# Decoder stage: the self-attention's small products placed beside the value products, its output projection one step later

## The chip, the cores and the metric

One core of a Trainium2 chip runs the whole program. The metric is device time in microseconds of one execution; the kernel before was timed in 3 runs, and a change is judged by the median.

## What is computed

The reference is a stack of four blocks over x (32 sequences of 32 rows, 256 wide) and a context of 257 rows a sequence. The change touches one part, the call `_L1_xattn_ref`: a decoder of six layers. Each layer does self-attention over the 32 rows (16 heads of 16, masked), adds and normalises, cross-attention to the context, adds and normalises, and a dense part of 256 to 1024 to 256 with ReLU, adds and normalises. In the reference's words, for a layer l:

```
x = layer_norm(x + mha(x, x, sa_w[l], sa_b[l], mask))
x = layer_norm(x + mha(x, ctx, ca_w[l], ca_b[l], None))
x = layer_norm(x + relu(x @ w1[l] + b1[l]) @ w2[l] + b2[l])
```

Everything is float32.

## The kernel before

`decoder_layers` (L2118) works on tiles of 128 rows, four sequences each: 8 tiles times 6 layers are 48 positions. A software pipeline runs over steps. In a step five parts work on different positions (L2179): `sa` (self-attention) on position step, `prep` (queries, keys and values of the cross-attention) on step - 1, `ca` (its scores, softmax, products) on step - 2, `out` (its projection) and `dm` (the dense part) on step - 3. So 51 steps; in the first three and the last three some parts are empty.

A step has eight units, u0 to u7. In every even unit PE does the scores of two units of four heads and sequences (L2359), DVE takes the row maximum from PSUM (`maxima`, L2454), ACT does four exponentials (`exponentials`, L2601), DVE forms reciprocal rates in the odd unit (`pair_rates`, L2460), POOL scales the probabilities (`scale`, L2539), and two units after its own each unit is transposed on PE (job T, L2371) and copied by ACT. In every odd unit PE multiplies a pair with the values (job PV, L2378), which DVE takes (`own_heads`, L2468).

Between these stand the jobs of the table `UNIT_JOBS` (L2133), each with the engine that evacuates its PSUM bank: `n`, `q`, `K`, `V`, `X` for prep (X, the last key's values, only in the first position of a layer), `Y` for out; `S0` transposes the input of self-attention, `S1q` and `S1k` are its queries and keys, `S2` its values, `S3` its scores, `S6` its products with the values, `S7` its output projection; `D0` to `D3` are the dense part: D0 transposes, D1 and D2 are the two halves of the first product, D3 is the second. All jobs, T and PV among them, go in one list in that order, T first in its unit and PV last (L2189). They share a ring of four PSUM banks, and a job waits for the evacuation of the job four before it (L2280):

```
o = ps[:, RING + n % RB]
if n >= RB:
    pe.wait_ge(s[evacuated[n - RB][0]], evacuated[n - RB][1])
```

Every engine does its part of this list in order, with its own work written between. DVE's loop (L2502): it first takes what it put off in the unit before (S3, D3 and PV), then the maximum in an even unit, then in u0 the unfinished norms, in u4 `self_shares` (sum, reciprocal, product and transpose of the self-attention's probabilities, L2493), in odd units the rates, then the jobs of the unit, then in u2 `own_queries` (L2478) and in u3 `self_shift` (mask, maximum, subtraction, L2486), then unfinished norms, save in u7. S2's evacuation (L2438) writes a masked copy of four times its size, and S1q's (L2432) one of eight times. A norm is `norm_statistics` (L2402), a root on POOL (`root`, L2535), and `norm_apply` (L2412). ACT's loop (L2609) takes in even units T and, save in u6, the first job behind it, then the exponentials, then the rest; in odd units its jobs; and in u3, behind these, the exponential of the self-attention (L2621). SP loads the next context tile in each step and the next layer's weights in groups, each behind the last use of the old ones (L2243).

The matmul forms differ: most products use the whole array (128x128). The scores use parts of 32 rows and 64 columns; S3 (L2330), S6 (L2338) and PV (L2386) use column strips of 32 ("128*32" in the profile), four at once.

Of the kernel before, what the change touches and what calls it, by code (L numbers as in the profile page):

```python
# [16 lines left out]
ACT = mybir.ActivationFunctionType  # L17
# [2100 lines left out]
def decoder_layers(E, A):  # L2118
# [8 lines left out]
    def k_job(i):  # L2127
        return ("K", (i // 2, i % 2), "act")

    def v_job(i):  # L2130
        return ("V", i, "dve")

    UNIT_JOBS = [  # L2133
        [("S0", None, "act"), k_job(0), v_job(0)],
        [("S1q", None, "dve"), k_job(1), ("S1k", None, "act"), ("n", None, "act")],
        [("q", None, "act"), v_job(1), ("Y", None, "dve"), ("S3", None, "dve")],
        [k_job(2), v_job(2)],
        [("D0", None, "act"), k_job(3), ("S2", None, "dve")],
        [("D1", 0, "act"), v_job(3), ("S6", None, "dve")],
        [("D2", 1, "act"), ("X", None, "act")],  # L2140
        [("S7", None, "dve"), ("D3", None, "dve")],
    ]
    PART = {"n": "prep", "X": "prep", "q": "prep", "K": "prep", "V": "prep", "Y": "out", "S0": "sa", "S1q": "sa", "S1k": "sa", "S2": "sa", "S3": "sa", "S6": "sa", "S7": "sa",
            "D0": "dm", "D1": "dm", "D2": "dm", "D3": "dm"}

    w = E.layer
# [8 lines left out]
    with ExitStack() as st:  # L2155
        s, handles = signals(st, nc, "layers", "job_done evac_dve evac_act scores_done max_ready exp_done "
                             "last_exp rates_ready scaled bias_ready shifted soft_done pT_ready qblk_ready h_sa h_ca h_dm var_ready added_eps power_ready dve_step "
                             "ctx0 ctx1 w_sa_qk w_sa_v w_sa_o w_ca_q w_ca_k w_ca_v w_ca_o w_dm")
# [5 lines left out]
        KT, V = sb("KT", [2, DC, GB * KW]), sb("V", [2, VC, D])  # L2164
# [5 lines left out]
        sa_sc, sa_pT, sa_attnT = sb("sa_sc", [16, LQ]), sb("sa_pT", [16 * LQ]), sb("sa_attnT", [DC, P])  # L2170
# [5 lines left out]
        NPOS = NL * NG  # L2176
        steps = []
        for step in range(NPOS + 3):
            at_part = {"sa": step, "prep": step - 1, "ca": step - 2, "out": step - 3, "dm": step - 3}  # L2179
            steps.append({part: pos if 0 <= pos < NPOS else None for part, pos in at_part.items()})  # L2180
        N = len(steps)

        def ca_unit(it):
            pos = it // U - 2
            if not 0 <= pos < NPOS:
                return None
            return it - 2 * U, pos, it % U // GB, it % GB

        jobs, at = [], {}  # L2189
        for step, parts in enumerate(steps):  # L2190
            for u in range(U):
                it = step * U + u
# [3 lines left out]
                for kind, arg, engine in UNIT_JOBS[u]:  # L2196
                    pos = parts[PART[kind]]
                    if pos is not None and (kind != "X" or pos % NG == 0):
# [14 lines left out]
        def jobs_in(it):  # L2213
            return by_unit.get(it, [])
# [19 lines left out]
        with nc.Block(no_gpsimd_drain=True) as blk:  # L2234
# [40 lines left out]
            def _(pe):  # L2275
                mm, tr = nc.tensor.matmul, nc.tensor.transpose

                def job(n, step, u, kind, arg, engine):
# [3 lines left out]
                    if kind in ("T", "PV"):  # L2282
                        (transposes if kind == "T" else values)(o, *ca_unit(arg)).then_inc(s["job_done"], 1)
                        return
                    pos = steps[step][PART[kind]]
                    tile = pos % NG
# [110 lines left out]
            def _(dve):  # L2397
# [14 lines left out]
                def norm_apply(kind, count, tile):  # L2412
                    y = ytmp[kind][:]
                    dve.wait_ge(s["power_ready"], count)
                    link(v.tensor_scalar(y, y, stats[kind][:, 6:7], stats[kind][:, 8:9], ALU.subtract, ALU.mult))
                    link(v.tensor_tensor(y, y, LN_ROWS[kind][:, 1], ALU.mult))
                    v.tensor_tensor(E.h[:, tile], y, LN_ROWS[kind][:, 2], ALU.add).then_inc(s["h_" + kind], 1)

                unfinished = []
# [73 lines left out]
                def self_shares(pos):  # L2493
                    dve.wait_ge(s["soft_done"], pos + 1)
                    link(v.tensor_reduce(sa_sum[:], sa_sc[:], AX.X, ALU.add))
                    link(v.reciprocal(sa_sum[:], sa_sum[:]))
                    link(v.tensor_tensor(sa_sc[:], sa_sc[:], sa_sum[:].unsqueeze(2).to_broadcast([P, 16, LQ]), ALU.mult))
                    v.transpose(sa_pT[:], sa_sc[:].rearrange("p h k -> p (h k)")).then_inc(s["pT_ready"], 1)
# [3 lines left out]
                for it in range(N * U + 1):  # L2502
                    step, u = it // U, it % U
                    for a in put_off:
                        take(*a)
                    put_off.clear()
                    if it % 2 == 0 and ca_unit(it):
                        maxima(*ca_unit(it))
                    if u == 0:
                        for a in unfinished:  # L2510
                            norm_apply(*a)
                        unfinished.clear()
                    if u == 4 and steps[step]["sa"] is not None:
                        self_shares(steps[step]["sa"])
                    if it % 2 and ca_unit(it - 1):
                        pair_rates(*ca_unit(it - 1))
                    for a in jobs_in(it):
                        if a[3] in ("S3", "D3", "PV"):
                            put_off.append(a)
                        else:  # L2520
                            take(*a)
                    if u == 2 and steps[step]["prep"] is not None:
                        own_queries(steps[step]["prep"])
                    if u == 3 and steps[step]["sa"] is not None:
                        self_shift(steps[step]["sa"])
                    if u != 7:
                        for a in unfinished:
                            norm_apply(*a)
                        unfinished.clear()

            @blk.gpsimd
            def _(pool):
                made = [0]

                def root(kind):  # L2535
                    power(E, pool, s, made[0], stats[kind][:, 8:9], stats[kind][:, 7:8], 1e-12)
                    made[0] += 1

                def scale(k, pos, cc, j):  # L2539

                    pool.wait_ge(s["rates_ready"], k // 2 + 1)
                    at = slice(2 * (j % 2), 2 * (j % 2) + 2)
                    nc.gpsimd.tensor_tensor(probs[:, cc, j // 2, at], probs[:, cc, j // 2, at], rates[:, cc, j // 2, at].unsqueeze(2).to_broadcast([P, 2, KW]), ALU.mult).then_inc(s["scaled"], 1)  # L2543

                for it in range(N * U + 1):
                    step, u = it // U, it % U
                    if u == 0 and step and steps[step - 1]["dm"] is not None:
                        root("dm")
                    if u == 2 and step < N and steps[step]["out"] is not None:
                        root("ca")  # L2550
                    if it % 2 and ca_unit(it - 1):
                        scale(*ca_unit(it - 1))
                        scale(*ca_unit(it))
                    if u == 7 and steps[step]["sa"] is not None:
                        root("sa")

            @blk.scalar
            def _(act):
                a = nc.scalar.activation
# [41 lines left out]
                def exponentials(k, pos, cc, j):  # L2601
                    act.wait_ge(s["max_ready"], k // 2 + 1)
                    if k >= U:
                        need_job(act, k + 1 - U, "T")
                    for r in range(4):
                        a(probs[:, cc, j // 2, r], ps[:, r, 0:KW], ACT.Exp, bias=negmax[:, cc, j // 2, r:r + 1], accum_out=totals[:, cc, j // 2, r:r + 1]).then_inc(s["exp_done"], 1)  # L2606
                    a(last_e[:, cc, j // 2], negmax[:, cc, j // 2], ACT.Exp).then_inc(s["last_exp"], 1)

                for it in range(N * U):  # L2609
                    step, u = it // U, it % U  # L2610
                    early = 0
                    if it % 2 == 0 and ca_unit(it):
                        early = (u != 6) + (jobs_in(it)[0][3] == "T")
                        for b in jobs_in(it)[0:early]:
                            take(*b)
                        exponentials(*ca_unit(it))
                    for b in jobs_in(it)[early:]:
                        take(*b)
                    if steps[step]["sa"] is not None and u == 3:
                        act.wait_ge(s["shifted"], steps[step]["sa"] + 1)  # L2620
                        a(sa_sc[:], sa_sc[:], ACT.Exp).then_inc(s["soft_done"], 1)  # L2621

        end_round(nc, handles)

# [1209 lines left out]
```

## Time and profile before

| | |
|---|---|
| median of 3 runs | 4272.2 us (4267.39 to 4278.87) |
| the profiled execution's own time | 4274.82 us |
| its span, first to last instruction | 4272.7 us |
| mean granted TensorE clock, share of full | 0.936 |
| busy: PE, DVE, ACT, POOL | 3751.7, 2537.8, 1808.4, 738.1 us |
| the decoder's stretch | about 725 to 2655 us of the span |

Busy time counts instructions; matmuls overlap, so the time that a job costs PE is read from its first start to the first start of the next job. "Idle before, releaser" is the time for which an engine stood still ahead of an instruction and what ended it. PEld is the weight load, which runs ahead of the matmul that uses it. A granted clock of 1.00 is 2.4 GHz, 0.50 is 1.2 GHz.

### The profile page before, as it was taken

Reading aid. Unit: us, or ns where it says so; the run is one execution under the profiler, and the core shown is the slowest. Engines: PE = TensorE matmul, PEld = TensorE weight load, DVE = VectorE, ACT = ScalarE, POOL = GpSimd, SP = SyncE. Lnnn points to the kernel's source line nnn. Section 1 sums busy time; section 2 is a strip of 40 time slices with the busy share of each in tenths; the row PEclk is TensorE's granted clock in tenths of the full one; section 3 lists DMA queues with packets and bytes.
Section 4 is the critical chain, followed back from the end, with each engine's and each line's share of the span. In section 5 each row is a group of like instructions: output and inputs, shape, how many; then the busy total and the mean of one; then the engine's idle time right before and its main releaser. Section 6 shows DMA issues by size and latency. Waiting matters only on the chain. (4 is left out here: it accounts for less than half of the span.)

```text
span 4272.7 us, 99175 instructions
## 1 busy us (share of the span) xinstructions
PE 3751.7 (88%) x40748; PEld 2830.3 (66%) x40748; DVE 2537.8 (59%) x5335; ACT 1808.4 (42%) x4979; POOL 738.1 (17%) x960
## 2 busy tenths in 40 slices
PE   7986995999999999999999997679678879889866
PEld 5765884677777777777777775568445569555535
DVE  4444213677777777777777774731257757346545
ACT  2221321445545455545555553212176736256522
POOL 1100101222222222222222222020121100000000
PEclk9998997999999999999999998879889979999977
DMA  5221386001101101111101100138544410000001
GB/s 175 91 76 52 109 303 221 31 31 43 61 31 47 56 32 52 51 36 47 61 29 45 61 21 12 40 131 297 208 142 150 154 35 1 27 31 31 11 3 49
DMA packets 141630, 329.30 MB, mean 77 GB/s; under 512 B 35512, under 2 KB 93304, under 8 KB 121984
## 3 DMA queue, kind: packets, MB, share of 16 engines
q1 hardware_dynamic: 138112, 314.57, 21.8%
q0 software_dynamic: 3072, 8.39, 0.6%
q8 instruction: 327, 5.36, 0.5%
q14 instruction: 119, 0.97, 0.1%
HBM read 286.98 MB, written 23.33 MB: 73 GB/s over the span
## 5 line engine op out<-in xcount | busy, mean ns | idle before, releaser
L2543 POOL TENSOR_TENSOR layers_probs<-layers_probs,layers_rates 128x512 f32<-128x512 f32 x384 | 399.9, 1063 | 906.8 <-DVE layers_rates L2466 906.8
L2570 ACT COPY layers_pT<-banks 128x512 f32<-128x512 f32 x384 | 227.9, 594 | 460.4 <-PE banks L2375 460.4
L2606 ACT ACTIVATE layers_probs<-banks,layers_negmax 128x256 f32<-128x256 f32 x768 | 354.1, 476 | 106.3 <-DVE layers_negmax L2458 106.2
L2311 PE MATMUL banks<-weights_a,ctx_tiles 128*128 128x256 f32 x1536 | 367.7, 382 | 27.5 <-ACT layers_KT L2583 27.5
L2304 PE MATMUL banks<-ctx_tiles,weights_a 128*128 128x512 f32 x768 | 364.8, 598 | 0.0
L2311 PEld LDWEIGHTS banks<-weights_a,ctx_tiles 128*128 128x128 f32 x1536 | 284.4, 190 | 112.1 <-issue 46.3
L2375 PE MATMUL banks<-const,layers_probs 128*128 128x128 f32 x1536 | 244.0, 282 | 2.9 <-POOL layers_probs L2543 2.8
L2375 PEld LDWEIGHTS banks<-const,layers_probs 128*128 128x128 f32 x1536 | 172.4, 142 | 106.5 <-issue 78.4
L2457 DVE TENSOR_REDUCE layers_negmax<-banks 128x4 f32<-128x1024 f32 x192 | 233.6, 1216 | 4.1 <-PE banks L2368 1.6
L2436 DVE COPY layers_V<-banks 128x512 f32<-128x512 f32 x192 | 132.4, 689 | 149.6 <-PE banks L2311 149.2
L2583 ACT ACTIVATE layers_KT<-banks,layers_key_bias 128x512 f32<-128x512 f32 x192 | 133.0, 693 | 154.1 <-PE banks L2304 153.9
L2304 PEld LDWEIGHTS banks<-ctx_tiles,weights_a 128*128 128x128 f32 x768 | 132.4, 192 | 93.8 <-issue 93.6
L2350 PE MATMUL banks<-layers_dm_nT,weights_b 128*128 128x128 f32 x1536 | 189.9, 278 | 0.6 <-ACT layers_dm_nT L2575 0.6
L2356 PE MATMUL banks<-weights_b,layers_hid 128*128 128x256 f32 x768 | 184.2, 385 | 4.5 <-ACT layers_hid L2598 4.2
L2350 PEld LDWEIGHTS banks<-layers_dm_nT,weights_b 128*128 128x128 f32 x1536 | 181.9, 194 | 0.9 <-ACT layers_dm_nT L2575 0.9
L2356 PEld LDWEIGHTS banks<-weights_b,layers_hid 128*128 128x128 f32 x768 | 141.8, 190 | 39.5 <-ACT layers_hid L2598 22.3
L2606 ACT ACTIVATION_READ_ACCUMULATOR layers_probs<-banks,layers_negmax 128x1 f32 x768 | 159.3, 207 | 0.0
L2368 PE MATMUL banks<-layers_KT,layers_qblk 32*64 32x256 f32 x3072 | 133.4, 403 | 0.0
L2386 PE MATMUL banks<-layers_pT,layers_V 128*32 128x64 f32 x6144 | 124.8, 222 | 9.2 <-ACT layers_pT L2570 7.7
L2886 PE MATMUL banks<-weights_a,ctx_tiles 128*128 128x512 f32 x256 | 128.8, 633 | 0.5
L2386 PEld LDWEIGHTS banks<-layers_pT,layers_V 128*32 128x32 f32 x6144 | 96.2, 110 | 49.6 <-issue 33.5
L2432 DVE SCALAR_TENSOR_TENSOR weights_a<-banks,layers_sa_cols,const 128x1024 f32<-128x1024 f32 x96 | 118.9, 1279 | 5.3 <-PE banks L2297 3.6
(707 smaller groups left out, 8126.9 us busy)
## 6 DMA issues: line engine op xcount, KB each, us to landing
ctx_tiles<-ctx_rel SPq DMA_DIRECT2D x48, 1024.0 KB, 5.7
weights_a<-in_L_w SPq DMA_DIRECT2D x44, 1024.0 KB, 5.6
l2x_B<-positions SPq DMA_DIRECT2D x32, 1280.0 KB, 5.8
weights_b<-in_L_w SPq DMA_DIRECT2D x32, 1024.0 KB, 6.4
ctx_tiles<-in_ctx SPq DMA_DIRECT2D x16, 1028.0 KB, 5.1
weights_c<-in_L_w SPq DMA_DIRECT2D x16, 1024.0 KB, 7.1
weights_b<-in_L_xattn_w SPq DMA_DIRECT2D x12, 1024.0 KB, 7.3
l0x_key_rows<-in_ctx_rows SPq DMA_DIRECT2D x32, 256.0 KB, 2.7
```

The source lines that it names most:

```text
L2304: last = mm(o, ca_wk[:, c, m * P:(m + 1) * P], E.ctx[:, tile % 2, c, 2 * i * KW:2 * (i + 1) * KW], start=c == 0, stop=c == DC - 1)
L2311: last = mm(o[:, b * D:(b + 1) * D], E.ctx[:, tile % 2, c, first:first + P], ca_wv[:, c], start=c == 0, stop=c == DC - 1)
L2350: last = mm(o[:, i * P:(i + 1) * P], dm_w1[:, c, m * P:(m + 1) * P], dm_nT[:, c], start=c == 0, stop=c == DC - 1)
L2356: last = mm(o[:, 0:D], hid[:, m], dm_w2[:, m], start=m == 0, stop=m == FC - 1)
L2368: last = mm(ps[64 * a:64 * (a + 1), r, 0:KW], qblk[rows, tile % 2, cc, j + a], KT[rows, tile % 2, cc, (j + a) * KW:(j + a + 1) * KW], star ...
L2375: last = tr(o[:, (KC * i + c) * P:(KC * i + c + 1) * P], probs[:, cc, j // 2, 2 * (j % 2) + i, c * P:(c + 1) * P], E.c("ident"))
L2386: last = mm(o[32 * r:32 * (r + 1), a * 64:(a + 1) * 64], V[:, pos % 2, KC * (j + a) + c, cc * P + 32 * r:cc * P + 32 * (r + 1)], pT[:, (k ...
L2457: link(v.tensor_reduce(peak, ps[:, 0:4, 0:KW], AX.X, ALU.max, negate=True))
L2543: nc.gpsimd.tensor_tensor(probs[:, cc, j // 2, at], probs[:, cc, j // 2, at], rates[:, cc, j // 2, at].unsqueeze(2).to_broadcast([P, 2, KW ...
L2570: nc.scalar.copy(pT[:, k % 4].rearrange("p t c x -> p (t c x)"), o).then_inc(s["evac_act"], 1)
L2583: last = a(KT[:, pos % 2, m, 2 * i * KW:2 * (i + 1) * KW], o, ACT.Identity, bias=key_bias[:, m:m + 1])
L2606: a(probs[:, cc, j // 2, r], ps[:, r, 0:KW], ACT.Exp, bias=negmax[:, cc, j // 2, r:r + 1], accum_out=totals[:, cc, j // 2, r:r + 1]).then_ ...
```

## The change

The table of jobs changes: S2 goes from u4 to u2, S3 from u2 to u3, S6 from u5 to u7, n from u1 to u2, q from u2 to u3, D3 ahead of S6 in u7, and S7 from u7 to u0 of the next step, behind K0, under a part name of its own, `sa_end` (position step - 1). S3 and S6 are now the last jobs ahead of the values' PV in u3 and u7. DVE puts S6 off as well; `own_queries` goes to u3, `self_shift` to u4, `self_shares` to u5 and behind the jobs of that unit; norms are finished in u7 too. POOL's root for the self-attention goes to u0, ACT's exponential of the self-attention to u5, behind T and ahead of the other jobs.

```diff
--- before.py
+++ after.py
@@ -2131,16 +2131,16 @@
         return ("V", i, "dve")
 
     UNIT_JOBS = [
-        [("S0", None, "act"), k_job(0), v_job(0)],
-        [("S1q", None, "dve"), k_job(1), ("S1k", None, "act"), ("n", None, "act")],
-        [("q", None, "act"), v_job(1), ("Y", None, "dve"), ("S3", None, "dve")],
-        [k_job(2), v_job(2)],
-        [("D0", None, "act"), k_job(3), ("S2", None, "dve")],
-        [("D1", 0, "act"), v_job(3), ("S6", None, "dve")],
+        [("S0", None, "act"), k_job(0), ("S7", None, "dve"), v_job(0)],
+        [("S1q", None, "dve"), k_job(1), ("S1k", None, "act")],
+        [("n", None, "act"), v_job(1), ("Y", None, "dve"), ("S2", None, "dve")],
+        [("q", None, "act"), k_job(2), v_job(2), ("S3", None, "dve")],
+        [("D0", None, "act"), k_job(3)],
+        [("D1", 0, "act"), v_job(3)],
         [("D2", 1, "act"), ("X", None, "act")],
-        [("S7", None, "dve"), ("D3", None, "dve")],
+        [("D3", None, "dve"), ("S6", None, "dve")],
     ]
-    PART = {"n": "prep", "X": "prep", "q": "prep", "K": "prep", "V": "prep", "Y": "out", "S0": "sa", "S1q": "sa", "S1k": "sa", "S2": "sa", "S3": "sa", "S6": "sa", "S7": "sa",
+    PART = {"n": "prep", "X": "prep", "q": "prep", "K": "prep", "V": "prep", "Y": "out", "S0": "sa", "S1q": "sa", "S1k": "sa", "S2": "sa", "S3": "sa", "S6": "sa", "S7": "sa_end",
             "D0": "dm", "D1": "dm", "D2": "dm", "D3": "dm"}
 
     w = E.layer
@@ -2176,7 +2176,7 @@
         NPOS = NL * NG
         steps = []
         for step in range(NPOS + 3):
-            at_part = {"sa": step, "prep": step - 1, "ca": step - 2, "out": step - 3, "dm": step - 3}
+            at_part = {"sa": step, "sa_end": step - 1, "prep": step - 1, "ca": step - 2, "out": step - 3, "dm": step - 3}
             steps.append({part: pos if 0 <= pos < NPOS else None for part, pos in at_part.items()})
         N = len(steps)
 
@@ -2510,23 +2510,22 @@
                         for a in unfinished:
                             norm_apply(*a)
                         unfinished.clear()
-                    if u == 4 and steps[step]["sa"] is not None:
-                        self_shares(steps[step]["sa"])
                     if it % 2 and ca_unit(it - 1):
                         pair_rates(*ca_unit(it - 1))
                     for a in jobs_in(it):
-                        if a[3] in ("S3", "D3", "PV"):
+                        if a[3] in ("S3", "S6", "D3", "PV"):
                             put_off.append(a)
                         else:
                             take(*a)
-                    if u == 2 and steps[step]["prep"] is not None:
+                    if u == 3 and steps[step]["prep"] is not None:
                         own_queries(steps[step]["prep"])
-                    if u == 3 and steps[step]["sa"] is not None:
+                    if u == 4 and steps[step]["sa"] is not None:
                         self_shift(steps[step]["sa"])
-                    if u != 7:
-                        for a in unfinished:
-                            norm_apply(*a)
-                        unfinished.clear()
+                    if u == 5 and steps[step]["sa"] is not None:
+                        self_shares(steps[step]["sa"])
+                    for a in unfinished:
+                        norm_apply(*a)
+                    unfinished.clear()
 
             @blk.gpsimd
             def _(pool):
@@ -2546,13 +2545,13 @@
                     step, u = it // U, it % U
                     if u == 0 and step and steps[step - 1]["dm"] is not None:
                         root("dm")
+                    if u == 0 and step < N and steps[step]["sa_end"] is not None:
+                        root("sa")
                     if u == 2 and step < N and steps[step]["out"] is not None:
                         root("ca")
                     if it % 2 and ca_unit(it - 1):
                         scale(*ca_unit(it - 1))
                         scale(*ca_unit(it))
-                    if u == 7 and steps[step]["sa"] is not None:
-                        root("sa")
 
             @blk.scalar
             def _(act):
@@ -2614,11 +2613,14 @@
                         for b in jobs_in(it)[0:early]:
                             take(*b)
                         exponentials(*ca_unit(it))
+                    if u == 5 and steps[step]["sa"] is not None:
+                        early = int(jobs_in(it)[:1] != [] and jobs_in(it)[0][3] == "T")
+                        for b in jobs_in(it)[0:early]:
+                            take(*b)
+                        act.wait_ge(s["shifted"], steps[step]["sa"] + 1)
+                        a(sa_sc[:], sa_sc[:], ACT.Exp).then_inc(s["soft_done"], 1)
                     for b in jobs_in(it)[early:]:
                         take(*b)
-                    if steps[step]["sa"] is not None and u == 3:
-                        act.wait_ge(s["shifted"], steps[step]["sa"] + 1)
-                        a(sa_sc[:], sa_sc[:], ACT.Exp).then_inc(s["soft_done"], 1)
 
         end_round(nc, handles)
 
```

## Rows read from the trace of the kernel before

**Rows 1.** Windows, one steady step: stretch, length, busy time (instructions) by engine, clock, DMA.

```profile
1513.53:1552.33 38.80, 38.19 (x449) 28.35 (x443) 30.01 (x67) 19.56 (x64) 10.79 (x15) 1.00 0.08 29
```

**Rows 2.** Waits, 760 to 2560 us: us in total, times, longest.

```profile
PE banks L2311 <- ACT layers_KT L2583: 27.5, 45, 0.6
```

**Rows 3.** Timeline of PE, part of a step: start, us, line, operation, instructions.

```profile
1526.87 1.03 PE L2320 MATMUL banks<-weights_a,layers_attnT 128*128 128x256 f32 x4
1527.83 1.07 PE L2330 MATMUL banks<-weights_a,layers_sa_k 128*32 128x256 f32 x16
...
1529.32 1.88 PE L2304 MATMUL banks<-ctx_tiles,weights_a 128*128 128x512 f32 x4
...
1537.79 1.95 PE L2350 MATMUL banks<-layers_dm_nT,weights_b 128*128 128x128 f32 x16
1540.36 1.99 PE L2311 MATMUL banks<-weights_a,ctx_tiles 128*128 128x256 f32 x8 [0.61 <-ACT layers_KT L2583]
1542.28 1.10 PE L2338 MATMUL banks<-layers_sa_pT,layers_sa_v 128*32 128x64 f32 x64
...
1543.76 0.69 PE L2368 MATMUL banks<-layers_KT,layers_qblk 32*64 32x256 f32 x16
...
1544.87 1.95 PE L2350 MATMUL banks<-layers_dm_nT,weights_b 128*128 128x128 f32 x16
1546.65 0.60 PE L2375 MATMUL banks<-const,layers_probs 128*128 128x128 f32 x4
1547.09 1.03 PE L2343 MATMUL banks<-weights_c,layers_sa_attnT 128*128 128x256 f32 x4
1547.96 3.85 PE L2356 MATMUL banks<-weights_b,layers_hid 128*128 128x256 f32 x16
1551.74 0.65 PE L2386 MATMUL banks<-layers_pT,layers_V 128*32 128x64 f32 x32
1552.33 0.69 PE L2368 MATMUL banks<-layers_KT,layers_qblk 32*64 32x256 f32 x16
...
1553.65 0.59 PE L2304 MATMUL banks<-ctx_tiles,weights_a 128*128 128x512 f32 x1
```

**Rows 4.** Timeline of the weight loads, D3's second half.

```profile
1549.82 1.59 PEld L2356 LDWEIGHTS banks<-weights_b,layers_hid 128*128 128x128 f32 x8 [0.37 <-ACT layers_hid L2598]
```

**Rows 5.** Timeline of DVE in the same step.

```profile
1513.05 0.42 DVE L2404 TENSOR_TENSOR layers_y_dm<-banks,rows_b 128x256 f32<-128x256 f32 x1 [0.56 <-PE banks L2356]
...
1514.53 0.25 DVE L2475 SCALAR_TENSOR_TENSOR layers_blend<-banks,const,layers_last_v 128x64 f32<-128x64 f32 x1
...
1537.57 0.68 DVE L2495 TENSOR_REDUCE layers_sa_sum<-layers_sa_sc 128x16 f32<-128x512 f32 x1
...
1539.93 1.18 DVE L2438 TENSOR_TENSOR layers_sa_v<-banks,const 128x1024 f32<-128x1024 f32 x1
...
1542.39 0.69 DVE L2436 COPY layers_V<-banks 128x512 f32<-128x512 f32 x1 [0.99 <-PE banks L2311]
1543.45 0.73 DVE L2444 TENSOR_SCALAR layers_sa_blend<-banks,const,layers_sa_bv 128x128 f32<-128x128 f32 x2 [0.37 <-PE banks L2338]
...
1544.74 0.27 DVE L2475 SCALAR_TENSOR_TENSOR layers_blend<-banks,const,layers_last_v 128x64 f32<-128x64 f32 x1
...
1545.25 1.21 DVE L2457 TENSOR_REDUCE layers_negmax<-banks 128x4 f32<-128x1024 f32 x1
```

**Rows 6.** Waits of PE, 724 to 853 us, where the pipeline fills.

```profile
PE banks L2338 <- DVE layers_sa_v L2438: 10.2, 3, 5.5
```

**Rows 7.** Windows of 5 us from the start of a gap on PE (clock is PEclk).

```profile
800.50:805.50 5.00, 3.25 (x122) 2.77 (x122) 4.49 (x12) 1.19 (x5) 2.04 (x2) 1.00 0.64 213
2665.60:2670.60 5.00, 2.30 (x15) 1.82 (x15) 3.36 (x7) 1.48 (x3) 0.79 (x2) 1.00 0.19 48
3132.10:3137.10 5.00, 2.88 (x46) 2.34 (x48) 2.99 (x2) 3.34 (x3) 0.00 (x0) 0.72 0.41 123
806.30:811.30 5.00, 1.99 (x51) 1.15 (x51) 2.66 (x9) 2.50 (x10) 2.03 (x2) 0.86 0.00 0
```

## The prediction, made before the changed kernel was run

> Places are named as in the code: a step is one position of the pipeline, u0 to u7 are its eight units, T3 is the transposes' job of u3, K3 and V3 are the key and value jobs by their numbers.
>
> **What bounds it now.** The windows view of one steady step gives its length, 38.80 us, and PE busy for 38.19 of it at full clock (2.4 GHz), with DVE at 30.01, ACT at 19.56 and POOL at 10.79 [rows 1]. So PE sets the step, the others matter only where PE waits for them, and a gain must be a PE wait or PE work that goes. The waits view has one such wait in every full step: V3 behind the evacuation of K3, 45 times [rows 2]. The timeline of PE then prices each job from its start to the next one's [rows 3]. D2 (16 products) takes 1.78 [rows 3]; D1, the same work, takes 2.57, so V3 starts 0.79 late, and it runs 1.92 where eight products at S7's 0.87 / 4 and 0.09 for what follows make 1.83: 0.88 in all. D3 takes 3.78 against 16 such products, 3.57: 0.21 is a wait for D2's evacuation, which the weight load of D3's second half shows as 0.37 of its own idle time [rows 4].
>
> **V3's wait goes.** A job needs the ring slot of the job four before it. V3's is K3's now (K3, S2, T, D1, V3); K3 is copied by ACT only behind the four exponentials. With S2 out of u4 the slot is D0's, evacuated ahead of the exponentials. Gain 0.88 a step. What is late next there is K3's slot, wanted by the value products of u5, a whole V3 later: no wait.
>
> **S3 moves beside the value products of u3.** Y before it takes 0.96 where S7, the same shape, takes 0.87: 0.09 for entering the 128x32 form. From S3 to K2, past T3, is 1.49 [rows 3]; less a T of 0.44, S3 and both its edges are 1.05, where its 16 instructions in four column strips are 4 x 0.2175 = 0.87. S6 with its values beside it takes 1.48, the values alone 0.59 [rows 3], so a neighbour of that form costs no edge. Gain 0.09 + 1.05 - 0.89 = 0.25, bounds 0.14 and 0.34. S6 gains nothing: it stands beside value products already. The Trainium skill, "TensorEngine Tiling (Array Packing)", Key Properties, says that changing the tiling mode drains the array, which these edges bear out; by that rule alone the change would take 12 us off. The same page, PSUM Bottleneck, warns that tiled products can leave the evacuation as the bound, which speaks against the change; K0's wait below is of that kind, and no row here shows it yet.
>
> **D3 waits for D2's evacuation.** This decides. D2 is copied by ACT behind the exponentials of u6, which wait for DVE's maximum of the same unit. What DVE does between V3 and that maximum changes. Now: V3's copy, S6's evacuation, the values', with the four operations of self_shares done before V3. After: V3's copy, then self_shares (which moved behind the jobs of u5), then the values'. By DVE's rows [rows 5]: 0.11 from V3's last product, copy 0.60 (0.69, of which the next operation covers 0.09), self_shares 2.36 (1537.57 to 1539.93), values 0.51: 3.58. From the start of the maximum to the weights of D3's second half are 4.57 us (1545.25 [rows 5] to 1549.82 [rows 4]), all of it that maximum, four exponentials and four copies, none of which the change touches. Released at 8.15 after V3. PE now has less to do in that time, for S6 no longer stands ahead of it and S7 no longer ahead of D3: values 0.59, scores and T6 1.11, D2 1.78, T7 0.44, eight products of D3 1.74, less 0.11 by which weights lead: 5.55 [rows 3]. Wait: 2.60. The check by differences: 0.21 now, 0.6 more on DVE, 1.76 less on PE (S6 1.48 - 0.59, S7 0.87), 2.57. The wait shows as some 2.3 us of idle PE, since pipelined ends cover the rest, as V3's 0.88 shows as 0.61. Loss 2.60 a step, bounds 2.2 and 3.0 by the overlap of rows. Nothing ahead excludes a gain but these two sums, which differ by far more than their parts are unsure.
>
> **The next step's first units.** DVE takes D3, S6 and the values one after another before the maximum of u0. S6 starts 1.48 before the scores of u0; D3's statistics begin 0.11 later and take 1.48 (1513.05 to 1514.53), S6's evacuation 1.29 (1543.45 to 1544.74) [rows 5], ending 1.40 to 1.48 after the scores' start. K0, four jobs behind S6 in the ring, would start 1.32 after it (scores and T 1.11, S0 some 0.2) with weights 0.11 earlier. Loss 0.3, bounds 0 and 0.5. T2's slot becomes S1q's (it was K1's), and S1q's evacuation, 2.5 us for two operations, now ends a run of DVE work that holds S7's statistics and finish as well: 0 to 0.4, taken as 0.1, since PE is itself 0.3 later.
>
> **What costs nothing, with its cover.** S7 keeps its 0.87 of PE; its slot and its input need S6's evacuation, by then done under K0. Its norm waits for POOL's root, now in u0 behind D3's root and ahead of u1's scaling; n, its only near reader, starts in u2, some 3 us after. If that cover went, PE would wait in n. The self-attention's exponential moves on ACT from u3, where it holds up the copy of T4, to behind T5's copy, and delays D1's evacuation by its 0.6; the user is D2's slot, over 1 us away. On SP the last weight group of a layer waits for h_sa, now some 8 us into the next step, with the next 1 MB context load queued behind it; that load is needed a step later. own_queries moves with q by one unit and has the rest of the step. No instruction or transfer is added.
>
> **Sum of a full step:** -0.88 - 0.21 - 0.25 + 2.60 + 0.3 + 0.1 = +1.66, so 40.5. Full steps are those with scores, self-attention and dense part, 45 by [rows 2]: +75. In five of them X (8 products, half of D2: 0.89) falls under the D3 wait: -4. In the three filling steps S6 waits 10.2 us for S2's evacuation behind self_shares [rows 6]; S2 now goes first and S6 later: 0 to -10, taken as -5. Together +66.
>
> **The clock.** An idle stretch can bring the clock to 1.2 GHz. Over 5 us from the start of a gap the rows show [rows 7]: gap 1.75 (5.00 less PE's 3.25), clock 1.00; gap 2.70, 1.00; gap 2.12, 0.72; gap 3.01, 0.86 and still low at the end. D3's gap of 2.3 stands 45 times among these. A drop costs 0.28 x 5 = 1.4, of which 0.1 lies under K0's wait. I take it in half of the steps, between the two that fell and the two that didn't: 22 x 1.3 = +29, bounds 0 and 45 x 1.4 = +63.
>
> **Against the measured time.** The profiled execution took 4274.8 us for its span of 4272.7; the median of the runs is 4272.2, so differences are added to that: 4272 + 66 + 29 = 4367.
>
> **Rivals.** (a) As forecast, but the gap leaves the clock alone: 4338. For it: the gap of 2.70. Against: that of 2.12. (b) The clock falls in nearly every step: 4272 + 66 + 63 = 4401. (c) Faster: DVE reaches the maximum of u6 in time, so D3 doesn't wait. The mechanism is the order on DVE in u5 and u6: it decides at 5.55 us from V3 to D3's second weights; if the shares were through before V3, as they are now, 2.36 of the 8.15 would go and the wait would shrink to 0.24; were it nothing, the step would be 38.80 - 1.34 + 0.4 = 37.9, times 45 -42, with the filling -47: 4225. For it: the exponential is ready before V3 is, and DVE then idles. Against: the diff puts self_shares behind the jobs, and engines run in order. (d) The waits only change places and the edges of S3 alone are left: -0.25 x 48 = 4260; this is the result that the page's rule on modes would give here. Against: two unequal sums in D3's wait.
>
> **Chances.** Forecast (clock falls in some steps) 0.60; (a) 0.20; (b) 0.11; (c) 0.06; (d) or a near balance 0.03. A measurement of this kernel tells 0.3%, some 13 us, from no change. So slower 0.91, same 0.03, faster 0.06. The range goes from (a) less 10 for the bounds of the D3 wait to (b) and a little: 4326 to 4409.
>
> **What would show it.** Right: a steady step of 40.5 or more; PE idle before L2356 for ACT L2598 of about 2.3 us, 45 times; none before L2311 in u5; L2457 of u6 straight behind L2475 and L2476, those behind L2498; PE's clock below 1.00 in the steady stretch; K0 (L2304) waiting about 0.3 for DVE L2447. Wrong: D2's evacuation ending before the eighth product of D3, which would mean that DVE or ACT doesn't keep its order or that V3 ends over 2 us sooner against D3 than I have it.

## Result, and the profile after

| | before | after |
|---|---|---|
| median of 5 runs | 4268.2 us | 4361.02 us (4353.48 to 4367.45) |
| ratio | | 1.0206, 95% interval 1.019 to 1.0221 |
| span of the profiled execution | 4272.7 us | 4351.7 us |
| steady step, first S3 to next S3 | 38.80 us | 40.25 us, but 41.6 to 42.2 in 19 steps |
| mean clock of the span, of full | 0.936 | 0.932 |

The kernel before has two more runs here than the three given with it. The medians alone give a ratio of 1.0217; the table has the recorded one with its interval.

The change made the kernel slower by 2.1%, 93 us. Forecast were 4367 us, 95 more.

The waits view of the changed kernel has one wait of PE in the steady stretch, and it isn't the one of [rows 2], which is gone (us in total, times, longest):

```profile
PE banks L2356 <- ACT layers_hid L2597: 99.8, 45, 2.3
```

Once in each of the 45 full steps, D3's second half waits for ACT's copies of D2: 2.31 us in 40 of them, 1.46 in the five where X lies under the wait. The timeline of PE, one step (start, us, line, operation):

```profile
1561.84 1.07 PE L2330 MATMUL banks<-weights_a,layers_sa_k 128*32 128x256 f32 x16
1562.73 0.63 PE L2386 MATMUL banks<-layers_pT,layers_V 128*32 128x64 f32 x32
1563.29 0.69 PE L2368 MATMUL banks<-layers_KT,layers_qblk 32*64 32x256 f32 x16
...
1570.39 0.65 PE L2386 MATMUL banks<-layers_pT,layers_V 128*32 128x64 f32 x32
...
1573.87 0.60 PE L2375 MATMUL banks<-const,layers_probs 128*128 128x128 f32 x4
1574.30 1.89 PE L2356 MATMUL banks<-weights_b,layers_hid 128*128 128x256 f32 x8
1578.51 1.99 PE L2356 MATMUL banks<-weights_b,layers_hid 128*128 128x256 f32 x8 [2.31 <-ACT layers_hid L2597]
1580.43 1.10 PE L2338 MATMUL banks<-layers_sa_pT,layers_sa_v 128*32 128x64 f32 x64
...
1581.91 0.69 PE L2368 MATMUL banks<-layers_KT,layers_qblk 32*64 32x256 f32 x16
...
1583.02 0.38 PE L2290 MATMUL banks<-const,h_state 128*128 128x128 f32 x2
1583.41 1.98 PE L2304 MATMUL banks<-ctx_tiles,weights_a 128*128 128x512 f32 x4
1585.24 1.03 PE L2343 MATMUL banks<-weights_c,layers_sa_attnT 128*128 128x256 f32 x4
...
1602.10 1.07 PE L2330 MATMUL banks<-weights_a,layers_sa_k 128*32 128x256 f32 x16
```

From S3 (1561.84) to the next S3 (1602.10) are 40.26. D3 is now two rows: eight instructions, 2.31 idle, eight more. From its start to S6's are 6.13, where its 16 instructions and what follows need 3.57: a wait of 2.56. In the next step's first unit K0 starts 0.39 after S0's transposes where 0.22 is usual, and runs to S7 in 1.83, where K jobs take 1.72: 0.28 for S6's evacuation. S3 beside the values takes 0.89 (1561.84 to 1562.73) and the values 0.56.

DVE in the same step:

```profile
1570.49 0.69 DVE L2436 COPY layers_V<-banks 128x512 f32<-128x512 f32 x1 [2.19 <-PE banks L2311]
1571.10 0.68 DVE L2495 TENSOR_REDUCE layers_sa_sum<-layers_sa_sc 128x16 f32<-128x512 f32 x1
...
1572.83 0.71 DVE L2498 STREAM_TRANSPOSE layers_sa_pT<-layers_sa_sc 128x512 f32<-128x512 f32 x1
1573.46 0.24 DVE L2475 SCALAR_TENSOR_TENSOR layers_blend<-banks,const,layers_last_v 128x64 f32<-128x64 f32 x1
...
1573.94 1.21 DVE L2457 TENSOR_REDUCE layers_negmax<-banks 128x4 f32<-128x1024 f32 x1
```

V3's copy, then self_shares, then the values', then the maximum, back to back. [Rows 5] had the maximum 2.86 us after V3's copy began, with the shares done before; here it is 3.45 after. ACT takes the exponentials from 1575.39 and D2's copies behind them:

```profile
1575.39 0.47 ACT L2605 ACTIVATE layers_probs<-banks,layers_negmax 128x256 f32<-128x256 f32 x1 [2.53 <-DVE layers_negmax L2458]
...
1577.30 1.15 ACT L2597 ACTIVATE layers_hid<-banks,layers_dm_cols 128x128 f32<-128x128 f32 x4
```

D2's products had ended by 1573.87, where T7 starts; its copies begin 3.4 us later. And the clock (windows: stretch, length, busy time and instructions by engine, clock): the same wait in this step and what follows it in the step before.

```profile
1574.30:1580.40 6.10, 3.79 (x18) 2.78 (x16) 1.36 (x4) 3.54 (x14) 2.04 (x2) 1.00 0.13 51
1536.60:1541.70 5.10, 5.10 (x111) 3.95 (x111) 1.31 (x4) 0.42 (x1) 1.50 (x2) 0.67 0.00 0
```

The gap of 2.31 leaves the clock at 1.00 in the first; after the same gap ending at 1536.60 PE works the next 5.1 us at 0.67 of full. That happened after 19 of the 40 gaps of 2.31, and after none of the five of 1.46. Steps in which it happens are 1.3 to 1.7 us longer.

### The profile page after: what moved, and what is told of

It is laid out like the page before. It is cut to its first block and busy times, and to the rows that moved or that the text cites. A ratio compares the mean times of both kernels' runs of the same rounds, so it can differ in the third digit from the quotient of the medians.

```text
span 4351.7 us, 99175 instructions
## 1 busy us (share of the span) xinstructions
PE 3758.7 (86%) x40748; PEld 2853.8 (66%) x40748; DVE 2505.3 (58%) x5335; ACT 1819.5 (42%) x4979; POOL 725.8 (17%) x960
## 5 line engine op out<-in xcount | busy, mean ns | idle before, releaser
L2542 POOL TENSOR_TENSOR layers_probs<-layers_probs,layers_rates 128x512 f32<-128x512 f32 x384 | 391.1, 1040 | 803.4 <-DVE layers_rates L2466 803.4
L2356 PE MATMUL banks<-weights_b,layers_hid 128*128 128x256 f32 x768 | 215.5, 431 | 100.1 <-ACT layers_hid L2597 99.8
L2356 PEld LDWEIGHTS banks<-weights_b,layers_hid 128*128 128x128 f32 x768 | 155.8, 213 | 140.6 <-ACT layers_hid L2597 118.9
```

The lines of the kernel that those rows point to most:

```text
L2356: last = mm(o[:, 0:D], hid[:, m], dm_w2[:, m], start=m == 0, stop=m == FC - 1)
```

## Experiments

Each kernel is compared with the kernel before on the same chip. "Step" is the steady step by its profiled execution. The groups ran on three chips, on which the median of the kernel before was 4277.1 (e1 to e4), 4274.5 (b1, b2, e5, e6) and 4276.1 us (e7, e8), against 4268.2 beside the changed kernel. So medians of different groups can differ by some 9 us for that alone; ratios and steps are the safer comparison.

| kernel | median us | ratio to before, 95% | step | idle before D3's second half |
|---|---|---|---|---|
| changed kernel | 4361.0 | 1.0206 (1.019 to 1.0221) | 40.25 | 2.31 |
| e1_shares_u6 | 4232.6 | 0.9908 (0.9884 to 0.9931) | 38.09 | none |
| e2_shares_before_v3 | 4280.9 | 1.0015 (1.0003 to 1.0028) | 39.19 | 1.25 |
| e3_fill_gap | 4331.9 | 1.0138 (1.0113 to 1.0163) | 40.25 | 0.58 |
| e4_s6_before_d3 | 4291.7 | 1.0043 (1.0025 to 1.006) | 39.07 | 1.08 |
| b1_s2_early | 4255.1 | 0.9955 (0.9941 to 0.9969) | 38.43 | none |
| b2_s7_next_step | 4323.9 | 1.0119 (1.0102 to 1.0136) | 40.12 | 0.84 |
| e5_s3_apart | 4244.7 | 0.9927 (0.9911 to 0.9944) | 38.38 | none |
| e6_s6_before_d3 | 4269.9 | 0.9989 (0.998 to 0.9999) | 39.02 | none |
| e8_d2_before_exp | 4240.0 | 0.9917 (0.9899 to 0.9935) | 38.13 | none |
| e7_both_orders | 4220.6 | 0.9878 (0.9856 to 0.99) | 37.84 | none |

### Is it DVE's order? e1 and e2

e1 moves self_shares to behind the maximum of u6:

```diff
                     if it % 2 == 0 and ca_unit(it):
                         maxima(*ca_unit(it))
+                    if u == 6 and steps[step]["sa"] is not None:
+                        self_shares(steps[step]["sa"])
...
-                    if u == 5 and steps[step]["sa"] is not None:
-                        self_shares(steps[step]["sa"])
```

> The changed kernel with self_shares moved on DVE from u5 to behind the maximum of u6; nothing else. Theory (DVE's order sets D3's wait): the maximum of u6 comes 2.36 us earlier, D2's evacuation with it, the wait of D3 shrinks from 2.60 to some 0.24 us (shown as idle: 2.31 to about 0), the steady step from 40.25 to 37.9, and no gap is left that lowers the clock: 4361 - 45 x 2.36 - 30 for the clock = 4225 us, below both kernels. Rival 1 (ACT itself or the dense part is late, whatever DVE does): 4361. Rival 2 (the shares in u6 delay the rates of u7 or S6 instead): idle of PE before L2375 or L2338, 4260 or more.

Measured 4232.6, step 38.09: 2.16 of the 2.36 came. PE's timeline has D3 in one row again, and DVE's has the maximum 1.27 behind the start of V3's copy (1522.47):

```profile
1526.28 4.04 PE L2356 MATMUL banks<-weights_b,layers_hid 128*128 128x256 f32 x16
```

```profile
1522.47 0.69 DVE L2436 COPY layers_V<-banks 128x512 f32<-128x512 f32 x1 [2.20 <-PE banks L2311]
...
1523.74 1.23 DVE L2457 TENSOR_REDUCE layers_negmax<-banks 128x4 f32<-128x1024 f32 x1
```

The missing 0.2 is left as a wait in D3, which takes 3.97 to S6 against 3.57. The rows put it down to the maximum, which now comes so early that it meets the scores of u6 themselves: PE began those at 1522.95, and the maximum begins 0.33 after the last operation on the values began, where it was 0.20. Rival 1 falls, and rival 2 too: nothing is late behind the moved shares. So the place of the shares alone turns a loss of 2.1% into a gain of 0.9%.

e2 moves them to ahead of the jobs of u5:

```diff
+                    if u == 5 and steps[step]["sa"] is not None:
+                        self_shares(steps[step]["sa"])
                     for a in jobs_in(it):
...
-                    if u == 5 and steps[step]["sa"] is not None:
-                        self_shares(steps[step]["sa"])
```

> The changed kernel with self_shares in u5 but ahead of the jobs, so ahead of V3's copy. The prediction's rival (c) took all 2.36 us off the chain: 4225. From the trace of the changed kernel ACT's exponential of the self-attention ends only 1.1 us before V3's last product, so the shares cannot be through by then: maximum of u6 1.1 us earlier, D3's wait 1.5 (shown as 1.2), step 39.1, clock at full: 4361 - 50 - 30 = 4281 us. If DVE's order didn't matter: 4361.

Measured 4280.9, step 39.19: only 1.06 less. DVE waits there for ACT's exponential:

```profile
1535.84 0.69 DVE L2495 TENSOR_REDUCE layers_sa_sum<-layers_sa_sc 128x16 f32<-128x512 f32 x1 [1.14 <-ACT layers_sa_sc L2621]
```

It is the same chain of 8.15 us, counted from V3, less the part of the shares that fits in ahead of V3's end. How much that is depends on when the exponential, on another engine, is through.

### The clock by itself: e3

```diff
                         need_evacuated(pe, pos, "D1", 0)
+                        for m in range(4):
+                            mm(o[:, 0:D], hid[:, m], dm_w2[:, m], start=m == 0, stop=m == 3)
                         for m in range(FC):
```

> The changed kernel with the first four of D3's eight products done twice, the second time overwriting the first: 8 more instructions, 1.74 us of PE work a step, under the wait of 2.60, with no change of result. It prices the clock by itself. Theory (a gap of 2.31 us lowers the clock in 19 of 45 steps): gap shown 0.6 us, clock 1.00 in the steady stretch, every full step 40.25, time 4361 - 30 = 4331 us. Rival 1 (the lowered clock costs nothing, since it falls under other waits): 4361. Rival 2 (the work isn't hidden): 4361 + 45 x 1.74 = 4439.

Measured 4331.9. The step is 40.25 in every full step, the gap 0.58, and the clock of the whole steady stretch 1.00 (the changed kernel has 0.98 there):

```profile
815.00:2530.00 1715.00, 1692.95 (x19170) 1288.30 (x19169) 1243.43 (x2808) 847.12 (x2747) 447.20 (x594) 1.00 0.14 44
```

So 384 more instructions, eight in each of 48 positions, make the kernel 29 us faster (by the medians, and by the two ratios as well). These 29 us are the clock's share of the loss; in the profiled execution it was 19 steps by some 1.6. What stays, 1.4% or some 59 us, is the longer step.

### What covered the wait: e4, b1, b2

e4 puts S6 ahead of D3:

```diff
-        [("D3", None, "dve"), ("S6", None, "dve")],
+        [("S6", None, "dve"), ("D3", None, "dve")],
```

> The changed kernel with S6 ahead of D3 in u7, so no longer beside the value products. Theory: D3's second half is released at the same time after V3, S6's 0.9 us of PE then lie under that wait, with its edges, and K0 no longer waits for S6's evacuation (0.29): step 40.25 - 0.89 - 0.29 = 39.1, gap shown about 1.3, clock at full: 4361 - 53 - 30 = 4278 us. Rival (the place beside the value products is worth more than what the wait hides): 4361 or slower, PE idle unchanged.

Step 39.07, as expected (39.1):

```profile
1505.26 1.10 PE L2338 MATMUL banks<-layers_sa_pT,layers_sa_v 128*32 128x64 f32 x64
1506.29 1.99 PE L2356 MATMUL banks<-weights_b,layers_hid 128*128 128x256 f32 x8
1509.37 1.99 PE L2356 MATMUL banks<-weights_b,layers_hid 128*128 128x256 f32 x8 [1.08 <-ACT layers_hid L2597]
```

S6 lies under the wait now, from 2.31 idle down to 1.08, and K0 no longer waits. The place beside the value products, for which S6 was moved, is worth less than the 0.9 of cover that it takes away. The time was 14 us over the expectation. Some 11 of that are the five steps with X, 1.7 to 3.4 longer: their gap is 2.16, and in two of them the clock fell. It is a cost of this order that I had not counted.

b1 takes the kernel before and moves S2 alone:

```diff
-        [("q", None, "act"), v_job(1), ("Y", None, "dve"), ("S3", None, "dve")],
+        [("q", None, "act"), v_job(1), ("Y", None, "dve"), ("S2", None, "dve"), ("S3", None, "dve")],
...
-        [("D0", None, "act"), k_job(3), ("S2", None, "dve")],
+        [("D0", None, "act"), k_job(3)],
```

> The kernel before with only S2 moved, from u4 to u2 behind Y. It takes the gain of V3's slot alone. Theory: V3's slot is D0's, so V3 no longer waits for K3's copy (0.88 a step), nothing else changes: step 38.80 to 37.92, idle of PE before L2311 gone, D3's small wait stays; 40 us less, ratio 0.991. Rival (the wait moves to the next job that needs ACT or DVE, D3's second half above all): 38.8, ratio 1.00.

V3's wait is gone, but the step is 38.43 where 37.92 was expected: 0.51 of the 0.88 is taken by a new wait (D1 starts 0.87 after T5 instead of 0.43, and takes 0.08 more). S2 had stood between K3 and T5 and had covered ACT: the self-attention's exponential (L2621, then still in u3) holds the copies of T4 and of D0 behind it, and D1 waits for the latter:

```profile
1530.51 0.63 ACT L2621 ACTIVATE layers_sa_sc<-layers_sa_sc 128x512 f32<-128x512 f32 x1 [3.91 <-DVE layers_sa_sc L2491]
...
1531.51 0.38 ACT L2575 COPY layers_dm_nT<-banks 128x256 f32<-128x256 f32 x1
```

```profile
1532.03 2.02 PE L2350 MATMUL banks<-layers_dm_nT,weights_b 128*128 128x128 f32 x16 [0.27 <-ACT layers_dm_nT L2575]
```

To have V3's gain whole, the exponential must not stand ahead of these copies. The change moves it behind T5's copy, and D1 there starts 0.44 after T5 again (1566.34 to 1566.78 in the changed kernel). The exponential's move by itself was not run. The shares must come after the exponential, but not right behind V3, where they make D3 wait: e1 has them later and keeps V3's gain.

b2 adds S7's move to b1, with its root on POOL and its norm on DVE (those lines are not shown here):

```diff
-        [("S0", None, "act"), k_job(0), v_job(0)],
+        [("S0", None, "act"), k_job(0), ("S7", None, "dve"), v_job(0)],
...
-        [("S7", None, "dve"), ("D3", None, "dve")],
+        [("D3", None, "dve")],
...
-            at_part = {"sa": step, "prep": step - 1, "ca": step - 2, "out": step - 3, "dm": step - 3}
+            at_part = {"sa": step, "sa_end": step - 1, "prep": step - 1, "ca": step - 2, "out": step - 3, "dm": step - 3}
```

> The kernel before with S2 in u2, as in b1_s2_early, and S7 moved as in the change, to u0 of the next step, with its root on POOL and its norm; S3, S6 and self_shares stay. It separates the two halves of D3's wait. Theory (S7's 0.87 us of PE stood between D2 and D3 and covered D2's evacuation): PE's work stays the same, D3's wait grows by 0.87 to some 1.1, the step is 37.92 + 0.87 = 38.8, ratio to the kernel before 1.00; the idle time shown before L2356 is some 0.8. Rival (only the place of self_shares matters): 37.9, ratio 0.991.

```profile
1528.26 1.99 PE L2356 MATMUL banks<-weights_b,layers_hid 128*128 128x256 f32 x8 [0.84 <-ACT layers_hid L2597]
...
1541.47 0.65 PE L2386 MATMUL banks<-layers_pT,layers_V 128*32 128x64 f32 x32 [0.75 <-DVE weights_a L2432]
```

The first row is D3's wait, 0.84 idle as expected (some 0.8): from D3's start at 1525.53 to the values at 1530.18 are 4.65, so 0.87 more than [rows 3] have with S7 in front. The second was not expected. The values of u1 need S1q's slot, as they did in the kernel before, but DVE now comes to S1q later. The evacuation, first in the kernel before, then in b2:

```profile
1558.63 2.48 DVE L2432 SCALAR_TENSOR_TENSOR weights_a<-banks,layers_sa_cols,const 128x1024 f32<-128x1024 f32 x2
```

```profile
1538.97 2.45 DVE L2432 SCALAR_TENSOR_TENSOR weights_a<-banks,layers_sa_cols,const 128x1024 f32<-128x1024 f32 x2
```

PE had begun S1q at 1557.54 and at 1536.84, so the evacuation starts 1.09 after it in the first and 2.13 in the second, where DVE has S7's addition and statistics in u0 as well. That costs 0.82, and 38.43 + 0.87 + 0.82 is the 40.12 measured. In the changed kernel the evacuation is as late (2.19) and the values of u1 don't wait: with n moved to u2 their slot is T1's. By the order of jobs that is what avoids the wait; no run tests n's place alone. The ratio missed for this reason, the tested half of the sum held.

### The edges of the tiling form: e5

e1 with S3 back at the end of u2:

```diff
-        [("n", None, "act"), v_job(1), ("Y", None, "dve"), ("S2", None, "dve")],
-        [("q", None, "act"), k_job(2), v_job(2), ("S3", None, "dve")],
+        [("n", None, "act"), v_job(1), ("Y", None, "dve"), ("S2", None, "dve"), ("S3", None, "dve")],
+        [("q", None, "act"), k_job(2), v_job(2)],
```

> e1_shares_u6 with S3 taken from its place beside the value products in u3 back to the end of u2. It prices the edges of the tiling form. Theory from the rows of before: 0.25 us a step, 38.09 to 38.34, 12 us, with no new idle time of PE; bounds 0.14 and 0.34. Rival (edges cost nothing, S3 is only another product): 38.09. A slot that comes late (V2 behind S3's evacuation) would show as idle time before L2311.

Step 38.38 against 38.09, no new idle time: 0.29 a step, which over 45 steps is 13 us. The medians (4244.7 and 4232.6, on different chips) differ by 12, the ratios by some 8. The intervals of the two ratios overlap; the steps, which repeat to 0.01, do not. What the change was named for works, and it is small.

### Better versions: e6, e8, e7

e6 puts S6 ahead of D3 in e1, with the edit of e4.

> e1_shares_u6 with S6 ahead of D3 in u7. Theory: S6's 0.9 us of PE cover what is left of D3's wait (0.4), K0 no longer waits for S6's evacuation (0.29), and the form's edges come back once (0.2): 38.09 to some 37.6, 20 us less than e1_shares_u6 but for the steps with X, which were slow in e4_s6_before_d3 and may take back 5 to 10. Rival (nothing is left to cover, the edges decide): 38.3.

This failed: step 39.02 where 37.6 was expected. With the shares in u6, S6's input is ready only behind them, and ahead of D3 it comes too soon:

```profile
1539.13 1.10 PE L2338 MATMUL banks<-layers_sa_pT,layers_sa_v 128*32 128x64 f32 x64 [1.22 <-DVE layers_sa_pT L2498]
```

e8 leaves the changed kernel's DVE alone and takes D2's evacuation ahead of the exponentials of u6 on ACT (it stood behind them in the kernel before too):

```diff
-                        early = (u != 6) + (jobs_in(it)[0][3] == "T")
+                        early = 1 + (jobs_in(it)[0][3] == "T")
```

> The changed kernel with one thing undone on ACT instead of DVE: in u6 D2's evacuation is taken ahead of the exponentials, as the first job is in the other even units; self_shares stays behind V3. Theory (D3 waits only because D2's evacuation stands behind exponentials that stand behind self_shares): D2's products end 1.5 us before the maximum does in the changed kernel's trace, so ACT does the four copies in time that it waits anyway; D3's wait of 2.60 is gone, nothing else is late, step 40.25 - 2.60 = 37.65, clock full: 4361 - 117 - 30 = 4214 us. Rival 1 (DVE is late for other users as well, the scaling for T0 or S6's input): idle before L2375 or L2338, 4240 or more. Rival 2 (exponentials are delayed by 1.2 us and the wait moves to u0): step 38.5.

D3's wait is gone, 4240.0, but the step is 38.13, not 37.65. PE:

```profile
1530.20 3.62 PE L2356 MATMUL banks<-weights_b,layers_hid 128*128 128x256 f32 x16
...
1537.19 1.98 PE L2304 MATMUL banks<-ctx_tiles,weights_a 128*128 128x512 f32 x4 [0.47 <-DVE layers_sa_attnT L2447]
```

K0's wait for S6's evacuation grew to 0.47 of idle time. DVE and POOL tell why:

```profile
1534.32 0.87 DVE L2406 TENSOR_TENSOR layers_y_dm<-layers_y_dm,h_state 128x256 f32<-128x256 f32 x1
```

```profile
1533.87 2.22 POOL L2542 TENSOR_TENSOR layers_probs<-layers_probs,layers_rates 128x512 f32<-128x512 f32 x2 [7.56 <-DVE layers_rates L2466]
```

L2406, with both inputs in SBUF, took 0.87 with POOL's scaling beside it, and 0.42 in the changed kernel (1581.00), where POOL was idle. As D3 ends sooner, its norm now meets the scaling. These 0.45 are what the step lacks: 40.25 - 2.58 + 0.45 = 38.12. In the kernel before, S7's norm met the scaling in the same way:

```profile
1549.55 1.05 DVE L2406 TENSOR_TENSOR layers_y_sa<-layers_y_sa,h_state 128x256 f32<-128x256 f32 x1
```

```profile
1549.29 2.22 POOL L2543 TENSOR_TENSOR layers_probs<-layers_probs,layers_rates 128x512 f32<-128x512 f32 x2 [5.78 <-DVE layers_rates L2466]
```

e7 has both orders, those of e1 and e8.

> e1_shares_u6 with D2's evacuation ahead of the exponentials of u6 as well. Theory: the rest of D3's wait (0.42) goes, step 38.09 - 0.42 = 37.67, 4214 us; the two orders each remove the same wait, so together they give no more than e8_d2_before_exp. Rival (here the maximum is ready before D2's products are, so the exponentials now wait for PE and everything behind them, rates and scaling for T0, comes about 2 us later): idle before L2375, step 38.1 or more.

4220.6, ratio 0.9878: 1.2% below the kernel before and the fastest of all. The step is 37.84. It gave more than e8, so the two orders are not quite the same gain:

```profile
1519.71 0.59 DVE L2406 TENSOR_TENSOR layers_y_dm<-layers_y_dm,h_state 128x256 f32<-128x256 f32 x1
```

```profile
1518.98 2.22 POOL L2542 TENSOR_TENSOR layers_probs<-layers_probs,layers_rates 128x512 f32<-128x512 f32 x2 [7.27 <-DVE layers_rates L2466]
```

The maximum is earlier here, so the exponentials, the rates and POOL's scaling are too, by 0.28 against D3's norm. L2406 loses only 0.17 to the scaling, K0 shows 0.18 of idle time, and 38.09 - 0.42 + 0.17 is the 37.84 measured.

## Why the prediction was right

**Bound and method.** PE sets the step and only its waits and work count: the steps measured come out as sums of PE's jobs and waits, with none left over above 0.02 where such a sum is given. Of the signs that the prediction named for being right, one failed: the plain step is 40.25 and not 40.5 or more.

**V3's wait.** Gone, as forecast. That it can't be had alone (b1) the prediction did not say; it listed ACT's exponential among the things that cost nothing, true for the whole change only.

**S3's edges.** Forecast 0.25, measured 0.29 (e5).

**D3's wait.** The deciding term: forecast 2.60, measured 2.56, shown as 2.31 of idle time where "some 2.3" was said. Its parts were tested one by one: the shares' 2.36 on DVE by e1 (2.16 came back), S7's 0.87 by b2, S6's 0.89 by e4.

**The next step's first units.** K0 0.3, measured 0.28. T2's 0.1 did not come: the 0.39 us that the trace books on its weight load as waiting for S1q's evacuation stood there in the kernel before as well, under another name (0.4, 45 times, behind n's copy), and PE lost nothing: T2 starts 0.62 after the scores in both. S7's norm ran on DVE away from POOL's scaling, so L2406 of it took 0.43 where it had 1.05.

**Sum of the step.** 40.5 forecast, 40.25 measured: -0.88 - 0.21 - 0.29 + 2.56 + 0.28 = +1.46.

**X.** Sized too small: 4 us forecast, some 8 measured. A pair of steps around X was 1.83 longer than two plain ones and is now 0.25 longer.

**Filling and draining.** This step of the prediction was wrong, and near in its sum by luck. It took 5 us off because S6 would no longer wait for S2's evacuation. But S6 then waits for the shares, 9.5 us in place of 10.2 (view of the changed kernel's waits, 724 to 853 us):

```profile
PE banks L2338 <- DVE layers_sa_pT L2498: 9.5, 3, 6.4
```

Filling, from the decoder's first product to the S3 of the first full step, is 0.8 us shorter. The emptying behind the last full step, of which the prediction said nothing, is some 4 shorter. The spans differ by 79: 65 for 45 steps by 1.45, 30 for the clock, less 8 for X, less these 5, less 3.5 outside the decoder, where the kernels are the same.

**The clock.** 22 steps by 1.3 forecast, 29 us; 19 by 1.6 measured in the profiled run, and 29 us by e3. The count was a guess between rows that said both; it was near by luck as much as by reason. That the runs lie 14 us apart goes with a clock of 0.927 to 0.932 over the span.

**The total.** 95 forecast, 93 between the medians, but 79 between the two profiled executions, and without the clock's share 66 forecast against some 59 (e3). So the total is nearer than its terms: the step was 0.2 too long and X too small in the forecast, and the profiled execution was the fastest of the five. In the others the clock over the span was lower or the same; how often it fell there isn't recorded.

**Rival (c)** was right in its mechanism and wrong in its arithmetic: it took all 2.36 off the chain by moving the shares ahead of V3. e2 shows 1.06, since the exponential isn't ready. Behind the maximum (e1) nearly the full gain is to be had, 2.16.

## What to carry to other kernels

When a job is moved for the sake of its neighbour, write down what it covered in its old place: here 1.8 us of PE between D2 and the half that reads it, worth six times the edges saved. In a software pipeline with in-order engines, follow each evacuation back through what stands ahead of it on its engine, and that through its own wait; the sum of such a chain against PE's work in the same stretch gave the wait to 0.04 us. Put work that nobody needs yet (here the shares) behind the short operation that starts the longest chain.

## What the runs showed of the hardware

A gap of 2.31 us on PE lowered the clock in 19 of 40 steps of the changed kernel (0.67 over the next 5.1 us) and left it at 1.00 in 21. So its length alone doesn't decide, and no run shows what else does. A gap of 2.16 (e4, steps with X) lowered it in two of five; gaps of 1.46 (changed kernel, with X), 1.25, 1.08, 0.84 and 0.58 (e2, e4, b2, e3) never did. Each fall cost some 1.6 us. Filling the gap with useless products was faster here than idling (e3).

A float32 add on DVE with two SBUF inputs of 128x256 (L2406) takes 0.42 alone. With POOL's products of 128x512 running (1.04 each alone), it ended 1.32 us after the first product's start in three kernels, however late it had begun: 0.27, 0.44 and 0.73 after that start (kernel before, e8, e7), with 1.05, 0.87 and 0.59 in its row. It looks held until the product is through, rather than slowed in proportion. The add before it (L2404), with one input in PSUM, took 0.42 beside the same products in e8 and e7. The hold lengthened a wait of PE (K0 in e8 and e7).
